# First layer: the two DMAs of each maxima tile move from SyncE's list to ScalarE's queue

## What is computed

```
x = x + _L0_attn_ref(_layernorm(x), w_q, w_k, w_v, w_out, softmax_scale)
x = x + _L0_ffn_ref(_layernorm(x), kernel, input_scale, kernel_scale, bias)
x = x + _L1_attn_ref(_layernorm(x), w_in, w_out)        # causal, with ALiBi
x = x + _L1_ffn_ref(_layernorm(x), W, b, lora_down, lora_up, down_aux, up_aux)

def _L0_attn_ref(x, w_q, w_k, w_v, w_out, softmax_scale):
    q = (x @ w_q.T).reshape(B, S, N_HEADS, dk)
    k = x @ w_k.T
    v = x @ w_v.T
    scores = jnp.einsum('bshd,btd->bhst', q, k) * softmax_scale[0]
    attn = jax.nn.softmax(scores, axis=-1)
    out = jnp.einsum('bhst,btd->bshd', attn, v).reshape(B, S, D)
    return out @ w_out.T
```

## Time and profile before

| | |
|---|---|
| median of 3 runs | 3747.14 us (3730.3 to 3751.18) |
| profiled execution, its own time | 3731.37 us |
| its span, first to last instruction | 3729.6 us |
| busy: TensorE, VectorE, ScalarE, GpSimd | 93%, 80%, 67%, 57% of the span |
| stretch 200 to 1800 us (first layer, 29 batches of some 55.3 us) | TensorE 1502.98, VectorE 1468.59, ScalarE 1244.75, GpSimd 1079.51 us busy |

### The profile page before, as it was taken

How to read it: one execution, slowest core, us unless ns; L and a number is a source line. 1 busy time by engine, 2 the same in 40 slices (tenths; PEclk the granted TensorE clock), 3 DMA queues, 4 the chain that set the end, 5 groups by cost and what they waited for, 6 DMA issues and landing times. The chain is left out here.

```text
span 3729.6 us, 79324 instructions
## 1 busy us (share of the span) xinstructions
PE 3470.8 (93%) x26824; PEld 1953.8 (52%) x26824; DVE 2979.1 (80%) x8450; ACT 2488.9 (67%) x5347; POOL 2120.0 (57%) x2340
## 2 busy tenths in 40 slices
PE   5999999999999999999779999999999999999997
PEld 2444444444444444444345666666665666666664
DVE  5899999999999999999457777777776777777773
ACT  2777777777777777777535666666665665666663
POOL 2366667667667676666563555554554554454542
PEclk7999999999999999999979999999999999999997
DMA  4343433433434434433366677777667677677760
GB/s 120 72 78 82 90 71 83 94 66 83 97 64 88 91 69 86 88 76 76 88 119 116 124 126 136 121 123 138 121 124 129 114 122 136 113 125 138 122 103 30
DMA packets 251934, 376.45 MB, mean 101 GB/s; under 512 B 21930, under 2 KB 122448, under 8 KB 251264
## 3 DMA queue, kind: packets, MB, share of 16 engines
q1 hardware_dynamic: 249484, 369.28, 52.3%
q10 hardware_dynamic: 2048, 2.10, 0.3%
HBM read 223.97 MB, written 136.95 MB: 97 GB/s over the span
## 5 line engine op out<-in xcount | busy, mean ns | idle before, releaser
L679 DVE TENSOR_REDUCE maxima<-ps_max 128x1 f32<-128x512 f32 x2048 | 1272.6, 682 | 85.6 <-PE ps_max L443 81.9
L1520 DVE CUSTOM_DVE_ANT_0 ps_max<-ps_max,mask 128x512 f32<-128x512 f32 (+3 forms) x2048 | 962.8, 516 | 353.4 <-PE ps_max L1242 350.7
L574 ACT ACTIVATE probs<-ps_rest 128x512 f32<-128x512 f32 x2048 | 1073.4, 602 | 243.4 <-PE ps_rest L456 242.7
L1393 ACT ACTIVATE probs<-ps_rest 128x512 f32<-128x512 f32 (+3 forms) x2048 | 773.6, 436 | 457.9 <-PE ps_rest L1263 405.6
L443 PE MATMUL ps_max<-k_op,q_op 48*128 48x512 f32 x2048 | 733.5, 448 | 62.3 <-DVE maxima L679 51.7
L456 PE MATMUL ps_rest<-q_op,k_op 50*128 50x512 f32 x2048 | 734.1, 445 | 0.9 <-DVE o_rows L741 0.5
L443 PEld LDWEIGHTS ps_max<-k_op,q_op 48*128 48x128 f32 x2048 | 341.3, 186 | 544.7 <-DVE maxima L679 447.9
L1242 PE MATMUL ps_max<-k_op,q_op 51*128 51x512 f32 (+3 forms) x2048 | 564.2, 366 | 23.6 <-DVE maxima L1520 4.6
L1263 PE MATMUL ps_rest<-q_op,k_op 53*128 53x512 f32 (+3 forms) x2048 | 558.2, 365 | 26.4 <-DMA q_op<-mrows 24.7
L477 PE MATMUL ps_pv<-probs,v_op 128*32 128x512 f32 x4096 | 542.1, 605 | 1.0 <-ACT oT L586 1.0
L1242 PEld LDWEIGHTS ps_max<-k_op,q_op 51*128 51x128 f32 x2048 | 315.0, 188 | 164.4 <-DVE maxima L1520 88.0
(11 more groups left out here) (144 smaller groups left out, 5700.3 us busy)
## 6 DMA issues: line engine op xcount, KB each, us to landing
qk_parts<-qparts SPq DMA_DIRECT2D x192, 512.0 KB, 3.3
q_op<-qk_parts SPq DMA_DIRECT2D x384, 256.0 KB, 7.8
k_op<-qk_parts SPq DMA_DIRECT2D x192, 256.0 KB, 10.7
xin<-in_x SPq DMA_DIRECT2D x32, 512.0 KB, 4.6
xres<-in_x SPq DMA_DIRECT2D x32, 512.0 KB, 4.8
x_mid<-xo SPq DMA_DIRECT2D x32, 512.0 KB, 3.2
xin<-x_mid SPq DMA_DIRECT2D x32, 512.0 KB, 7.8
xres<-x_mid SPq DMA_DIRECT2D x32, 512.0 KB, 15.6
```

The costliest lines, as they stand in the source:

```text
L574: act.activation(probs[:, quad % 2, at:at + S], ps_rest[:, bank("exp", b, p), :], ACT.Exp).then_inc(ps_out["exp"], 1)
L679: dve.tensor_reduce(at, ps_max[:, bank("max", c, k), :], AX.X, ALU.max).then_inc(ps_out["max"], 1)
L1393: act.activation(probs[quad % 2][:, at:at + nq], ps_rest[:, bank("exp", b, p), 0:nq], ACT.Exp).then_inc(ps_out["exp"], 1)
L1520: dve.tensor_tensor_reduce(row, row, mask[:, S - keys:S], 1.0, LOWEST, ALU.add, ALU.max, at).then_inc(ps_out["max"], 1)
```

## The change

SyncE's list loses the steps `load_m`: the function that waited for the copy and issued the two DMAs is gone, and the words `load_m:...` of the plan no longer do anything. ScalarE's queue issues the same two DMAs, from the same rows to the same rows and with the same semaphore, directly behind the copy, after a wait for the copy itself. Nothing else moves.

```diff
-        def load_maxima(c, par, quad):
-            if not valid(c):
-                return
-            n = c * NQUAD + quad
-            sp.wait_ge(ps_out["m"], n + 1)
-            rows = HALF_ROWS * (quad // 2) + KA
-            first = QUAD * (quad % 2)
-            for r in range(M_ROWS):
-                sp.dma_start(q_op[rows + r:rows + r + 1, par, first:first + QUAD, :].bitcast(F32),
-                             mrows[r * QUAD:(r + 1) * QUAD, quad % 2, :].bitcast(F32)).then_inc(m_loaded, 16)
...
-                elif kind == "load_m":
-                    load_maxima(b + d, (par + d) % 2, k)
...
+        def send_maxima(c, par, quad):
+            act.wait_ge(ps_out["m"], c * NQUAD + quad + 1)
+            rows = HALF_ROWS * (quad // 2) + KA
+            first = QUAD * (quad % 2)
+            for r in range(M_ROWS):
+                act.dma_start(q_op[rows + r:rows + r + 1, par, first:first + QUAD, :].bitcast(F32),
+                              mrows[r * QUAD:(r + 1) * QUAD, quad % 2, :].bitcast(F32)).then_inc(m_loaded, 16)
...
             ins.then_inc(ps_out[kind], 1)
+            if kind == "m":
+                send_maxima(c, cp, k)
```

## The result

The changed kernel is slower: 3776.39 us against 3733.11 us, medians of 17 runs each, ratio 1.0111 with a 95% interval of 1.0086 to 1.0136. By that ratio it is 41 us more (43 as the difference of the medians), where 13.4 were forecast. "Slower by over 0.5%" had a chance of 0.28.

A forecast was written before the change was run, and what follows sets the result against it. TensorE and VectorE were taken to hand the lead to each other through the banks of `ps_max`, ScalarE following. 0.42 us x 32 batches at m:3, all else 0, gave 13.4 us: 3747.1 + 13.4 = 3760.5, given as 3760, range 3740 to 3782.

The forecast's parts named there:

- Slower by over 0.5%: Outcome of at least 18.7 us more than before, about what a measurement can tell from no change; chance 0.28.
- `m:3`: ScalarE's exponentials behind this copy of maxima start late, delaying TensorE's output product: 0.42 us a batch, 13.4 us in all.
- `m:1` and `m:2`: Behind these two copies of maxima, ScalarE's idle time covers the two DMA issues: price 0.
- `m:0`: Behind this copy, y and the first x_cols start 1.07 us later, but TensorE uses them several microseconds later: price 0.
- more than one place shows: Rival: m:0's delay also reaches TensorE; 31 us with half the 1.07 us, 54 us in full; chance 0.19.
- The DMAs themselves: The copy releases them on ScalarE's queue at the same moment as on SyncE's; rows land as early or earlier: 0.
- SyncE's list: SyncE loses 256 DMA issues and 128 waits, but nothing in the first layer waits for what becomes earlier: 0.
- The sum: Total over the places: 13.4 + 0 + 0 = 13.4 us, +0.36% on the profiled execution.

The follow-up runs named there:

- the gate at `m:3`: Changed kernel, GpSimd's last fp8 rounding sum waiting until VectorE has split m:3's maxima: ratio 1.0038 to before; the same wait in the kernel before: 0.9862.
- the gate at `m:1`: Changed kernel, with GpSimd's sum of finish:1 held until VectorE has split the maxima of m:1: ratio 1.0084 to the kernel before.

## Why the prediction was right and wrong

**`m:3`, 0.42 us: right.** Measured 0.45 to 0.47, with the two DMAs in 1.19 us, the exponential 1.26 us behind the copy, and the delay reaching TensorE at the bank of the product ahead of the output product. One detail was off: the profile names TensorE's exp tile, not the issue, as what released that exponential. The price holds for the kernel as it is; with the gate at `m:3` the same send costs 1.09.

**`m:1` and `m:2`, 0: right.** 12.72 and 15.12 us, and a ratio of 0.9998 for the two together.

**`m:0`, "Price 0, but with more steps than the others": the step that failed.** It measured 0.61 us a batch, 19.5 us, more than the whole forecast. The prediction followed the 1.07 us delay correctly from y to x_cols to GpSimd's split and the second x_cols, and then asked only when TensorE's banks would want them. Most of the delay went another way: GpSimd's instructions behind the split were all 0.8 us late, and one of them ran beside VectorE's split of `m:1`, which ends when that instruction does. VectorE is on the path there. The rows of the split were not among those that it stood on: no wait shows there, VectorE is busy, and one sees it only by asking what an instruction on 128 x 16 numbers should take.

The rival "more than one place shows" named the place and, with half of the 1.07 us, the size (31 us; the regular batches lost 33). Its condition, a bank that is wanted, was not the one that decided: by a bank came 0.17 to 0.19 us, and they show only with the gate at `m:1`. That its size fits is luck.

**The DMAs themselves, 0: nearly.** They are issued as early as before, but from another queue than the loads of `xres` and `q_op`, and the order between them is lost; "the rows land as early as before or earlier" does not hold in every batch. In the changed kernel this costs 4.7 us of waits between 100 and 1880 us, part of the 6 us in irregular batches; in its variants up to 28.8. Why the two DMAs behind `m:0` sometimes take 1.5 to 1.8 us is open.

**SyncE's list, 0: right as to the changed kernel.** Its waits moved to GpSimd as forecast, and nothing became earlier. Keeping the waits without the rows costs more, not less (1.0179 against 1.0111).

**The sum.** 14.4 us for `m:3` (0.45 x 32, where 13.4 were forecast), 19.5 for `m:0`, some 6 in irregular batches: 40 us, which agrees with the 39.7 us of the first layer's traces and with the timed 41. At least 2 of the 6 belong to the batch in which the clock fell, which no run ties to the change. The period was forecast at 55.7 us and is 56.4.

## What to carry to other kernels

Before moving DMA issues onto an engine that computes, follow the delay of each instruction behind them through every engine it feeds, to what runs beside the late ones and not only to what waits for them. Look in the profile for tiny instructions that take several times their usual duration: that is a wait that no list of waits shows, and here, at `m:3`, putting one semaphore ahead of a GpSimd instruction was worth 1.4%, while the change under study lost 1.1%. Where a small transfer holds up the lead, look at which large ones are issued around it: here it landed in time when one list issued it ahead of them, and on a queue of its own it had no such order.

## What the runs showed of the hardware

A VectorE instruction of 0.17 us (128 x 16) lasted 1.44 us in most batches at `m:3`, and up to 1.73, when a GpSimd instruction was running on its arrival, and ended 0.03 us behind that one; with the GpSimd instruction held back it took 0.16 to 0.18. The duration that the profile gives such an instruction holds the blocked time and counts as busy. The Trainium skill (SBUF — State Buffer, section "SBUF: two separate sides") says that VectorE and GpSimd share a port pair as an exclusive lock for a whole instruction, in which the loser is blocked fully, and names two cases: a VectorE instruction with two inputs from SBUF, and one in a 2-port performance mode. The trace agrees for the split's second instruction, which has two inputs. The first has one and was blocked as well; whether it ran in such a mode no run here shows.

A DMA issue held ScalarE's queue for 0.58 us at 8 KB and 0.62 at 16 KB, so between these two sizes the number of DMAs set the price, not their bytes.

Two rows of 8 KB on ScalarE's queue, issued together with, or up to 1.5 us behind, a load of 512 KB by SyncE and mostly ahead of three of 256 KB, landed late enough to stop TensorE 24 and 19 times, by 1.2 and 0.8 us on average (28.8 / 24 and 16.1 / 19), at most 3.4. The Trainium skill (DMA: Bandwidth & Descriptors, section "Queues, rings and completion order") says that each DMA engine takes turns between its queues a packet at a time. The waits agree with it in that a queue of their own did not spare the rows from the large loads. How the packets took turns no run here shows.
